# Perceiver block on one core: waits per tile and new cyclic orders in the context attention

## The reference, cut to what matters

```python
# x: (16, 64, 512), ctx: (16, 1601, 256); 16 heads of 32
q = layer_norm_per_head(x @ Wq + bq)
k = layer_norm_per_head(ctx @ Wk + bk)      # 1585 "main" keys; the last 16 go another way
v = ctx @ Wv + bv
out = softmax(q k^T / sqrt(32)) v           # per head, 64 queries, 1585 keys
x = x + (out + out_dca) @ Wo + bo
```

## Time and profile before

| | us |
|---|---|
| median of the runs | 3173.96 (3173.36 to 3180.48) |
| the profiled execution's own time | 3177.43 |
| its span, first to last instruction | 3175.6 |
| mean granted clock of TensorE, share of 2.4 GHz | 0.960 |
| context attention, layer 0: first k to last pv | 107.3 to 1133.6 |
| context attention, layer 1: first k to last pv | 1821.7 to 2847.8 |

### The profile page before, as it was taken

How to read it: one execution, slowest core, us unless ns; L and a number is a source line. 1 busy time by engine, 2 the same in 40 slices (tenths; PEclk the granted TensorE clock), 3 DMA queues, 4 the chain that set the end, 5 groups by cost and what they waited for, 6 DMA issues and landing times. The chain is left out here.

```text
span 3175.6 us, 86675 instructions
## 1 busy us (share of the span) xinstructions
PE 2894.2 (91%) x34089; PEld 1765.8 (56%) x34089; DVE 2585.9 (81%) x4082; ACT 2282.1 (72%) x4155; POOL 1619.6 (51%) x2006
## 2 busy tenths in 40 slices
PE   7799999999999878789996789999999999977889
PEld 3245555555555556577773335555555555554546
DVE  6699999999999756768875589999999999957752
ACT  5478998988998765346664459989988998973431
POOL 1256776776777542212223237767776776742210
PEclk9899999999999889889998899999999999989989
DMA  3344544444444343358894334444444444421010
GB/s 124 94 82 81 92 84 81 84 87 81 87 83 85 65 138 141 116 183 299 299 302 143 111 76 84 90 81 84 84 85 80 92 84 80 72 77 25 1 72 27
DMA packets 542685, 328.45 MB, mean 103 GB/s; under 512 B 459381, under 2 KB 504565, under 8 KB 536522
## 3 DMA queue, kind: packets, MB, share of 16 engines
q1 hardware_dynamic: 534314, 295.63, 40.4%
q0 software_dynamic: 7680, 25.17, 2.7%
q10 hardware_dynamic: 288, 2.10, 0.2%
HBM read 181.86 MB, written 36.09 MB: 69 GB/s over the span
## 5 line engine op out<-in xcount | busy, mean ns | idle before, releaser
L335 POOL TENSOR_TENSOR a_elo<-a_e 128x1024 f16<-128x1024 f32 x428 | 852.9, 1996 | 301.4 <-ACT a_e L422 297.7
L591 PE MATMUL a_ps_k<-l_wk,a_yh 128*128 128x512 f16 (+1 forms) x1664 | 574.0, 386 | 42.3 <-POOL a_yl L317 36.7
L591 PE MATMUL a_ps_v<-l_wv,a_yh 128*128 128x512 f16 (+1 forms) x1664 | 569.2, 383 | 12.2 <-DVE a_v L482 8.8
L493 DVE TENSOR_REDUCE a_mx<-a_ps_m 128x2 f32<-128x1024 f32 x384 | 467.7, 1218 | 11.4 <-PE a_ps_m L617 10.4
L420 ACT ACTIVATE a_e<-a_ps_t 128x1024 f32<-128x1024 f32 x428 | 410.6, 959 | 22.0 <-PE a_ps_t L651 16.7
L422 ACT ACTIVATE a_e<-a_ps_t 128x1024 f16<-128x1024 f32 x428 | 411.6, 962 | 0.0
L651 PE MATMUL a_ps_t<-a_qb,a_kk 64*128 64x128 f16 (+1 forms) x9672 | 350.5, 218 | 23.0 <-DVE a_qb L517 20.2
L675 PE MATMUL a_ps_o<-a_v,a_e 128*128 128x65 f16 (+1 forms) x3240 | 343.9, 193 | 13.0 <-POOL a_elo L335 12.8
L675 PEld LDWEIGHTS a_ps_o<-a_v,a_e 128*128 128x128 f16 (+1 forms) x3240 | 298.6, 96 | 98.5 <-issue 61.5
L651 PEld LDWEIGHTS a_ps_t<-a_qb,a_kk 64*128 64x128 f16 (+1 forms) x9672 | 286.4, 95 | 103.7 <-DVE a_qb L517 35.4
L677 PE MATMUL a_ps_o<-a_v,a_e 128*128 128x64 f16 (+1 forms) x3240 | 342.8, 194 | 0.0
(11 more groups left out here) (423 smaller groups left out, 5821.1 us busy)
## 6 DMA issues: line engine op xcount, KB each, us to landing
l_land<-in_ctx SPq DMA_DIRECT2D x96, 384.0 KB, 3.7
l_ob<-in_m_w SPq DMA_DIRECT2D x32, 1024.0 KB, 8.0
f_w<-in_m_w SPq DMA_DIRECT2D x32, 512.0 KB, 4.7
eo_dram<-f_e_eo SPq DMA_DIRECT2D x32, 512.0 KB, 4.4
l_land<-in_ctx SPq DMA_DIRECT2D x32, 433.0 KB, 3.9
a_kk<-a_khl SPq DMA_TRANSPOSE x416, 3.1
qs_dram<-p_q SPq DMA_DIRECT2D x32, 128.0 KB, 2.3
dca_dram<-p_od SPq DMA_DIRECT2D x16, 256.0 KB, 2.4
```

Of the source, the lines that this page charges most:

```text
L335: pool.tensor_tensor(rest[0:r, :, 0:w], full[0:r, :, 0:w], high[0:r, :, 0:w], ALU.subtract)\
L493: dve.tensor_reduce(mx[:, g, :, c], ps_m[:, :, :], AX.X, ALU.max).then_inc(mx_done, 1)
L591: m = pe.matmul(out[0:r, :], part[:, n % 2, c, cols], w[:, wpart, c, :], start=(c == 0 and a == 0), stop=(c == KC - 1 and a == 2))
```

## The change

Three waits are cut finer, the ring of K rows counts through all batches, and `ORDER` is replaced by another order of the same steps:

```diff
-            return (2 * at.nbp + i) % 4
+            return (at.nb * KT + i) % 4
...
                     sp.wait_ge(kl_done, n + 1)
-                    if i == 0 and b >= 2:
-                        sp.wait_ge(s_done, (b - 1) * UNITS)
+                    if b >= 2:
+                        sp.wait_ge(s_done, (b - 2) * UNITS + TPAIRS + i // 2 + 1)
...
                     act.wait_ge(v_done, n + 1)
-                    if i == 0 and at.nb >= 2:
-                        act.wait_ge(pv_done, 2 + (at.nb - 1) * UNITS)
+                    if at.nb >= 2:
+                        act.wait_ge(pv_done, 2 + (at.nb - 2) * UNITS + TPAIRS + i // 2 + 1)
...
                     dve.wait_ge(k_done, n + 1)
-                    need(dve, hat_done, n - 2 if i < 3 else n - 3)
+                    need(dve, hat_done, n - 3)
```

The new order (the old one is in the kernel's listing above and here, removed lines first):

```diff
-    PE: k12-- v8-- pv7-- s9-- m4-- pv8-- v9-- k0- s10-- m5-- v10-- k1- pv9-- m6-- s11-- v11-- pv10-- m7--
-    PE: s12-- k2- pv11-- m8-- v12-- m9-- s13-- pv12-- m10-- v0- pv13-- m11-- k3- m12-- v1- tb-- k4- v2- s0-
-    PE: k5- v3- s1- k6- v4- pv0- s2- k7- v5- pv1- s3- k8- v6- pv2- m0- s4- k9- pv3- m1- s5- k10- pv4- s6- v7-
-    PE: s7- pv5- m2- k11- pv6- s8- m3-
-    ACT: rp8-- vh7-- sq11-- e8-- kh8-- r5-- vh8-- yh0- rp9-- e9-- kh9-- vh9-- rp10-- sq12-- kh10-- e10--
-    ACT: rp11-- vh10-- r6-- kh11-- sq0- e11-- vh11-- rp12-- sq1- e12-- kh12-- r0- vh12-- e13-- yh1- sq2- rp0-
-    ACT: vh0- kh0- rp1- vh1- sq3- qh-- r1- kh1- vh2- yh2- e0- rp2- sq4- vh3- kh2- e1- sq5- rp3- sq6- vh4- r2-
-    ACT: kh3- e2- rp4- vh5- sq7- kh4- yh3- e3- rp5- vh6- r3- kh5- e4- sq8- rp6- sq9- e5- kh6- e6- rp7- sq10-
-    ACT: r4- kh7- e7-
-    DVE: kc2- m10-- hat0- m11-- vl0- kl0- m12-- t-- kc3- rd2- qs-- vl1- rd3- hat1- ql-- kc4- kl1- vl2- kc5-
-    DVE: hat2- rd4- vl3- kl2- o1-- kc6- rd5- hat3- vl4- rd6- kl3- kc7- hat4- vl5- rd7- kl4- kc8- hat5- vl6-
-    DVE: m0- kl5- kc9- hat6- rd8- m1- kc10- kl6- rd9- hat7- rd10- kl7- m2- kc11- hat8- vl7- o0- rd11- m3- kl8-
-    DVE: kc12- vl8- hat9- m4- kl9- vl9- hat10- kc0 m5- kl10- rd12- hat11- vl10- kc1 kl11- m6- rd0 m7- vl11-
-    DVE: rd1 hat12- m8- kl12- m9- vl12-
-    POOL: nw0- lo13-- yl1- nw1- yl2- qm- lo0- lo1- nw2- lo2- yl3- lo3- nw3- lo4- lo5- lo6- nw4- lo7- lo8- yl0
-    POOL: nw5- lo9- lo10- nw6- lo11- lo12-
+    PE: k12-- pv2-- s4-- m3-- v11-- pv3-- s5-- m4-- k0- pv4-- m5-- s6-- k1- v12-- pv5-- s7-- m6-- k2- pv6--
+    PE: s8-- m7-- v0- pv7-- k3- s9-- m8-- v1- pv8-- k4- m9-- v2- s10-- m10-- pv9-- v3- k5- s11-- m11-- v4-
+    PE: pv10-- m12-- s12-- k6- v5- k7- tb-- s13-- v6- k8- pv11-- v7- pv12-- s0- k9- pv13-- v8- s1- m0- k10-
+    PE: pv0- m1- s2- v9- pv1- k11- s3- m2- v10-
+    ACT: sq12-- rp10-- sq0- e6-- kh10-- vh12-- yh1- rp11-- e7-- kh11-- sq1- r6-- e8-- vh0- rp12-- sq2- r0-
+    ACT: e9-- kh12-- vh1- rp0- sq3- kh0- vh2- e10-- rp1- r1- vh3- yh2- kh1- sq4- e11-- vh4- rp2- sq5- e12--
+    ACT: kh2- vh5- r2- rp3- sq6- yh3- kh3- vh6- sq7- rp4- qh-- e13-- kh4- vh7- r3- sq8- rp5- e0- kh5- vh8- e1-
+    ACT: rp6- sq9- kh6- e2- sq10- rp7- vh9- yh0 r4- kh7- e3- rp8- vh10- sq11- kh8- e4- r5- rp9- vh11- e5- kh9-
+    DVE: hat9-- m4-- vl11-- kc0- kl9-- m5-- hat10-- rd12-- kc1- kl10-- rd0- hat11-- m6-- vl12-- kl11-- o0--
+    DVE: kc2- m7-- rd1- vl0- hat12-- rd2- kc3- m8-- kl12-- vl1- hat0- m9-- kl0- vl2- kc4- rd3- m10-- hat1-
+    DVE: vl3- kc5- m11-- rd4- kl1- m12-- vl4- hat2- t-- kc6- rd5- kl2- vl5- hat3- rd6- qs-- kc7- kl3- vl6-
+    DVE: rd7- hat4- ql-- kc8- kl4- vl7- rd8- hat5- kc9- o1-- kl5- vl8- m0- hat6- m1- kc10- kl6- rd9- hat7-
+    DVE: vl9- kc11- rd10- kl7- m2- hat8- vl10- rd11- kl8- m3- kc12-
+    POOL: lo8-- nw0- lo9-- lo10-- yl2- nw1- lo11-- qm- nw2- lo12-- yl3- lo13-- nw3- lo0- lo1- lo2- nw4- yl0
+    POOL: lo3- lo4- nw5- lo5- lo6- yl1 lo7- nw6-
```

## The result

The kernel with the change takes 3151.96 us (median of 5 runs, 3148.73 to 3160.18), beside 3174.82 for the kernel before (5 runs, 3173.36 to 3183.03): a ratio of 0.9925, 95% interval 0.9905 to 0.9946. It is faster by 23 us where 70 were forecast, and above the range. The profiled execution took 3156.05 us, with a span of 3154.2.

What follows compares the result with a forecast made beforehand. A loop through PE, ACT and DVE was taken to set the 61.3 us turn; 58.8 us over 14 turns a layer, ends 0, gave -70 in two layers: 3177.43 to 3107, median 3104 us, range 3084 to 3148.

Steps and rivals of the forecast that it cites:

- ql's price: VectorE's step making the low half of the query, priced at 0.87 us from the earlier trace, unchanged at its new place.
- the loop by the old course: The old limiting path through PE, ACT and DVE, followed in the new order: 58.0 us a turn.
- PE's wait for ql gone: Sign of being right: PE's 0.51 us idle before a batch's first score step vanishes.
- PE's sum of 58.35 us: PE's steps of one full turn laid end to end, the same in both orders: 58.35 us.
- the 0.3 allowed for loops: Added to each turn for loops through three engines, which cost 0.9 us in the old order: 0.3 us.
- Rival (b): PE's busy time in the attention stretches is the limit: 59.8 us a turn, 3132 to 3138 us; chance 7%.
- The waits: Three loosened waits and the longer ring, with the old order: a gain of 0 to 0.5 us a turn.
- The ends: Turns 0, 1, 16 and the tail of each layer: +1, -2, +1 and 0 us, in sum 0.
- Rival (a): POOL's queue, waiting in order, delays every turn by a further 1 us: 59.8 us a turn, 3132 us; chance 15%.
- Rival (d): PE's score steps wait for ACT's late exponentials; at 0.3 us each, 62.5 us a turn, 3208 us; chance 8%.
- Rival (e): Turns 0 and 1 run wholly at the lower PE clock, some 19 and 23 us more a layer: 3188; chance 2%.
- Rival (c): The new orders gain nothing: an unsummed loop holds turns near 61.3 us, ends cancel; 3165 to 3177 us; chance 6%.

## Why the prediction was wrong

**The step that failed is ql's price**, "m12, t, qs, ql" with the 0.87 us of the earlier trace rows, carried unchanged to a place where another engine is busy. It measured 2.63. The price is in the sum of DVE's 55.9 us, in the loop by the old course ("DVE from kl12 to ql", 58.0 us; with 1.76 more it is 59.8), and decisively in "PE's wait for ql gone": instead PE stands 1.10 us there. Taking the cause away and nothing else takes the turn from 60.40 to 59.26. So of the 1.6 us by which a turn of 60.4 misses 58.8, ql holds 1.1.

What the trace of before could have told: POOL's first nw row beside ql has 0.35 us, where the same instruction has 0.25 at other places of after's timeline. That could have been taken for a sign of something shared. The Trainium skill (SBUF — State Buffer, Who interferes with whom) states the rule: a VectorE instruction with two SBUF inputs takes its second one through a read interface that it shares with GpSimd, and so contends with a GpSimd instruction that reads SBUF; the shared ports are an exclusive lock, which whoever issues first has for the whole instruction. These runs agree: up to 1.99 us for a half of 0.48, and 0.47 to 0.49 with one input in PSUM. I had walked POOL's queue for its waits, but not asked what runs beside each step that has two inputs in SBUF.

**The second step is PE's sum of 58.35 us**, which was too small, and which the 0.3 allowed for loops did not make up. With ql repaired the turn is 59.26, 0.5 over the forecast and 0.9 over that sum, and PE has no wait left in it. Laid end to end from PE's timeline with q in PSUM, each step from its start to the next one's, the turn is k and v 35.1 us (summed as 33.8), m and m12 3.8 (3.0), s 9.4 (10.1), pv 10.4 (10.9), tb 0.6: 59.3. The prices were read from one row of each kind, and steps of a kind have two lengths. Thirteen of the k and v take 1.30 us and thirteen 1.39 to 1.41, all those ahead of scores or of tb among them; one of the twelve long m takes 0.23, ahead of an s, and the others 0.31 to 0.34:

```profile
559.97 0.38 PE L591 MATMUL a_ps_k<-l_wk,a_yh 128*128 128x512 f16 x1
...
561.37 0.84 PE L651 MATMUL a_ps_t<-a_qb,a_kk 64*128 64x128 f16 x24
562.05 0.38 PE L617 MATMUL a_ps_m<-a_kk,a_qm 64*128 64x512 f16 x2
562.36 0.39 PE L591 MATMUL a_ps_v<-l_wv,a_yh 128*128 128x512 f16 x1
```

A turn of before has both lengths too (nine of its k and v at 1.39 to 1.41, five of its m at 0.31 to 0.32), so this could have been read ahead. Whether the 0.1 us more is PE's own or a short wait under the tail, no run shows. Rival (b), which took PE's busy time as the limit, was thus nearly right on what lies under ql's wait: its 59.8 us a turn, from 894.7 us of 918.1, was 0.5 too high, since the new order takes PE 59.3 where the old one takes it 60.1 (the turn from 546.85 to 608.14). I gave it 7% with the argument that busy rows overlap.

**The sum of the miss.** Against the profiled executions, 3107 forecast and 3156.05 measured: 28 turns x (60.5 - 58.8) = 47.6 us; the ends -0.7 instead of 0 in each layer, -1.4; outside the attention +2.8, under the spread of the runs and not explained. Together 49.0.

**The waits**: right, and shown alone (0.2 us a turn, forecast 0 to 0.5).

**The ends**: right in sum, by luck: three of the four terms lie outside their bounds, and cancel. Turn 0 came to 45.9 us, +3.9 where +1 was forecast and +2 was the bound; turn 1 to 55.6, -7.2 (forecast -2, bound -4); turn 16 to 35.3, +5.2 (+1, bound +3); the tail to 30.1, -2.7 (0, bound -5). PE has 216 matmuls fewer in turn 1 and 197 more in turn 16 than before, so in the new order more of a batch's work stands behind the cut at k12, and passes from the one end to the other; turn 0 has hardly more work (144 matmuls for 128), and its 3.9 us are not explained. In the tail the granted clock was 1.00 where the earlier trace rows have 0.82, the gain that was named as possible. The single terms were not measured one by one.

**Rival (a)**, POOL's queue, came as near in time as (b) (59.8 us a turn). Its place is in the trace: qm waits 3.1 us for tb, as laid out. But it isn't what held after's turn: with q in PSUM the same wait of 3.1 us stands at a turn of 59.26. It comes forward once yl3 is made later, as the run with yl3 held shows.

**Rival (d)**, the exponentials: wrong. The waits of a turn of after have no s waiting for an e. **Rival (e)**, the clock: wrong, turn 0 was granted 0.88 and turn 1 1.00, no lower than the 0.86 and 0.95 before. **Rival (c)**, nothing gained: wrong, by 0.9 us a turn.

## What to carry to other kernels

When a step moves in a hand-written order, its duration has to be asked for again: for each VectorE instruction with two tensor inputs in SBUF, look at what GpSimd runs beside it at the new place, and add up to the rest of that instruction's time. Here one of the inputs could be left in PSUM, which took 27 us off the median for one added view and one changed wait. And one row is not enough to price a kind of step, as its length can go by its neighbour; when a sum of step lengths lies below an engine's measured busy time, keep the busy time as a bound with a fair chance, not as a remote one.

## What the runs showed of the hardware

- A VectorE instruction of 0.48 us with both tensor inputs in SBUF took up to 1.99 us beside GpSimd's elementwise work, and ended about 0.29 us after the end of a GpSimd instruction; with one input in PSUM it took 0.47 to 0.49 in all 64 cases at the same place.
- GpSimd pays too: the two instructions behind were 1.95 and 1.33 us beside ql, 1.79 and 1.16 where ql has one SBUF input.
- Beside five short GpSimd instructions (3.06 us in all, 0.6 each) each half of ql took 0.74 us instead of 0.48: beside shorter instructions the price was smaller.
- From its start to the next step's start, a K or V step (six matmuls of 512 columns, at a granted clock of 1.00) took either 1.30 us or 1.39 to 1.41, and always the longer ahead of a score step; two matmuls of 512 columns took 0.23 us, ahead of scores only, or 0.31 to 0.34. It is so in the kernel before and with q in PSUM.
